# One residual subtraction of the last query head is moved ahead of the projection's evictions on VectorE

## The reference, cut to what matters

```python
def _L0_xattn_ref(query, key, value, mask, wq, wk, wv, wo):
    q = (query @ wq).reshape(bs, s, N_Q_HEADS, D_K).transpose(0, 2, 1, 3)
    k = (key @ wk).reshape(bs, s, N_KV_HEADS, D_K).transpose(0, 2, 1, 3)
    v = (value @ wv).reshape(bs, s, N_KV_HEADS, D_V).transpose(0, 2, 1, 3)
    q = _rope(q)
    k = _rope(k)
    ...
    scores = jnp.einsum('bhgqd,bhkd->bhgqk', qg, k) / scale
    masked = jnp.where(mask[:, None, None].astype(bool), scores, -1000000000.0)
    w = jax.nn.softmax(masked, axis=-1)
    out = jnp.einsum('bhgqk,bhkd->bhgqd', w, v)
    ...
    return out @ wo
```

## Time and profile before

| | |
|---|---|
| runs | 2452.93, 2455.95, 2454.99 us; median 2454.99 us |
| profiled execution | 2452.93 us, its span 2451.1 us |
| PE busy | 2382.1 us (97%) |
| PE weight load | 1309.2 us (53%) |
| DVE busy | 1636.0 us (67%) |
| ACT busy | 1254.0 us (51%) |
| POOL busy | 1221.6 us (50%) |

### The profile page before, as it was taken

The page is one execution under the profiler, slowest core; times in us unless marked ns, Lnnn a source line. Parts: engine busy times, 40 slices in busy tenths (PEclk is TensorE's granted clock), DMA queues, the critical chain, the costliest instruction groups (busy, mean ns, idle before and its releaser), DMA issues.

```text
span 2451.1 us, 45213 instructions
## 1 busy us (share of the span) xinstructions
PE 2382.1 (97%) x17719; PEld 1309.2 (53%) x17719; DVE 1636.0 (67%) x3133; ACT 1254.0 (51%) x2425; POOL 1221.6 (50%) x981
## 2 busy tenths in 40 slices
PE   7799999999999999999999999999999999999998
PEld 4455555555555555444444555555555555555554
DVE  6877777777777788754443556667666666755666
ACT  6665555555565554423232554555454555544453
POOL 3566666666666666423222355544444445445541
PEclk9899999999999999999999999999999999999999
DMA  6011211112121111101000111122221212221101
GB/s 208 27 44 35 53 44 44 39 40 53 27 53 27 42 28 41 33 20 58 28 28 12 44 31 27 27 61 55 51 61 36 61 36 61 52 42 27 27 14 69
DMA packets 221554, 108.16 MB, mean 44 GB/s; under 512 B 174080, under 2 KB 197280, under 8 KB 221344
## 3 DMA queue, kind: packets, MB, share of 16 engines
q1 hardware_dynamic: 221344, 105.27, 17.0%
HBM read 61.62 MB, written 4.19 MB: 27 GB/s over the span
## 4 chain that ended last, share of the span: by engine, by line
PE 54%; DVE 4%; POOL 3%; ACT 1%; issue 1%; DVEq 0%; ACTq 0%; POOLq 0%
PE PB L854 14%; PE PB L806 12%; PE PB L966 9%; PE PB L790 6%; PE PB L983 5%; PE PB L831 2%; PE PB L896 2%; PE PB L875 1%; DVE AR L2108 1%; DVE SML L1919 1%; PE PB L1080 1%; PE PB L925 1%; POOL AR L2720 1%; POOL PSP L2699 0%; POOL AR L2681 0%
## 5 line engine op out<-in xcount | busy, mean ns | idle before, releaser
L854 PE MATMUL PB<-WB,AR 128*128 128x512 f16 x3072 | 690.8, 381 | 16.9 <-DVE X L2123 11.2
L806 PE MATMUL PB<-XTB,WB 128*128 128x512 f16 x3072 | 682.0, 379 | 3.4 <-ACT WB L1352 1.9
L854 PEld LDWEIGHTS PB<-WB,AR 128*128 128x128 f16 x3072 | 296.7, 98 | 379.6 <-DVE X L2123 21.8
L806 PEld LDWEIGHTS PB<-XTB,WB 128*128 128x128 f16 x3072 | 299.1, 98 | 342.0 <-issue 3.1
L2692 POOL TENSOR_TENSOR AR<-AR,SML 128x512 f32<-128x512 f32 x128 | 144.6, 1151 | 316.9 <-DVE SML L2093 316.9
L2123 DVE SCALAR_TENSOR_TENSOR X<-PB,SML,X 128x512 f32<-128x512 f32 x256 | 187.3, 748 | 163.9 <-PE PB L854 157.3
L1476 ACT ACTIVATE AR<-PB 128x512 f16<-128x512 f32 x256 | 131.6, 598 | 237.9 <-PE PB L896 237.8
L2681 POOL TENSOR_TENSOR AR<-AR,CST 128x512 f32<-128x512 f32 x128 | 181.6, 1418 | 44.1 <-ACT AR L1386 44.1
L2003 DVE TENSOR_TENSOR AR<-PB,AR 128x512 f16<-128x512 f32 x128 | 88.2, 690 | 170.3 <-ACT AR L1439 170.3
L966 PE MATMUL PB<-XTB,AR 128*128 128x512 f16 (+1 forms) x864 | 192.5, 379 | 0.0
L1974 DVE TENSOR_TENSOR AR<-AR 128x512 f16<-128x512 f32 x128 | 138.7, 1083 | 69.8 <-ACT AR L1392 69.4
(11 more groups left out here) (272 smaller groups left out, 3806.4 us busy)
## 6 DMA issues: line engine op xcount, KB each, us to landing
STG<-in_wo SPq DMA_DIRECT2D x14, 1024.0 KB
STG<-in_wq SPq DMA_DIRECT2D x13, 1024.0 KB
STG<-in_qw_gu SPq DMA_DIRECT2D x40, 128.0 KB
STG<-in_ctxT SPq DMA_DIRECT2D x4, 1024.0 KB
X<-in_x SPq DMA_DIRECT2D x4, 1024.0 KB, 10.8
out_x<-X SPq DMA_DIRECT2D x16, 256.0 KB, 2.5
AR<-PSP SPq DMA_TRANSPOSE x240, 2.4
STG<-in_wk SPq DMA_DIRECT2D x14, 256.0 KB
```

The lines of the kernel that those rows point to most:

```text
L806: m = pe.do.matmul(b[:, :], wq[x][:, k, h * 128:(h + 1) * 128], XT[y][c][:, k, :], start=n == 0, stop=n == 11)
L854: m = pe.do.matmul(b[:, :], AT[x][:, h, t * 128:(t + 1) * 128], wo[y][:, h, :], start=n == 0, stop=n == 11)
```

## The change

In the program of VectorE alone, in layer 0 alone, the low part of the last query head (h = 3) of the next unit is written after the first of the four evictions instead of after the third. The side stage of that slot, which stood behind it, now stands ahead of it. Nothing is added or taken away, and no other engine's program is touched.

```diff
                         if L and t == 2:
                             norm_q(u + 1)
-                        if L == 0 and t == 2:
+                        side(L, u, 5 + t)
+                        if L == 0 and t == 0:
                             queries_0(u + 1, 3)
-                        side(L, u, 5 + t)
                     side(L, u, 9)
```

## The result

The changed kernel takes 2485.62 us (2485.04 to 2486.96, 4 runs) against 2453.96 us before (2451.37 to 2455.95): 1.0133 of the time before, 95% interval 1.012 to 1.0145, or 31.7 us more. The forecast was 2490, in the range 2478 to 2502.

The account below looks back on a forecast made before the run. TensorE was taken to bound the kernel, so only its late starts cost time. Gain 0, cost 31.2 + 4.5 = 35.7 us on the profiled 2452.9, plus 2.1 for the median, gave 2490.7; forecast 2490, range 2478 to 2502.

Parts of the forecast that it names:

- The gain, nothing: Scores of layer 0: the low part was never late for them, so gain 0, bounded by 7.6 us.
- The cost of an ordinary unit, 1.46 us: Weigh in unit 13 starts 1.46 us later, waiting for bank 0 behind the delayed evictions of tiles 1 and 2.
- The sum: Layer 0: 31.2 us from units 6 to 27 plus 4.5 us from eight other units, +35.7 us.
- Does a late weigh get hidden later? No.: TensorE after weigh: scores and keys follow back to back, so the delay is not recovered.
- What comes back to TensorE starts from TensorE's own results: Turned heads, softmax and evictions start from TensorE's results, so they slip along with a late weigh.
- rival 1: Waits at tile 3 and in unit 2 shrink to nothing, giving back 11.2 us: +24.5, 2479 us; chance 0.07.
- No second wait: Keys on bank 2: tile 3's eviction frees it with 1.4 us margin, about 1 in units with wide residuals.
- The clock: TensorE's granted clock stays 1.00 despite the new waits at weigh.
- rival 3: TensorE's clock falls at each new wait, slowing weigh and scores: 2552 us, or 2518 with weigh alone; chance 0.02.
- rival 2: Delay at weigh is hidden because its bank is free 1.46 us earlier: no change, 2455 us; chance 0.03.
- rival 4: A second wait, for bank 2, in each ordinary unit: 2502 us; chance 0.05.
- rival 5: Scores wait unseen for head 3's low part; 7.6 us gained, no cost at weigh: 2447 us; chance 0.03.

Follow-up runs that it names:

- E4: Kernel before with head 3's low part after tile 3's eviction instead of after tile 2's: 2464.24 us, 1.0041 of before.
- E2: Changed kernel with the moved instruction after tile 1's eviction instead of after tile 0's: 2468.34 us, 1.006 of before.
- E7: Kernel before with GpSimd's first sine product of the keys waiting for VectorE's softmax subtractions in rounds 10, 14, 18, 22, 26: 2452.60 us, 0.9998.
- E1: Changed kernel with tile 2 of the layer 0 projection in PSUM bank 5 instead of bank 0, output units 0 to 29: 2481.69 us, 1.0114 of before.
- E5: Changed kernel with tile 2 of the layer 0 projection in PSUM bank 5 for output units 0 to 26 only: 2475.99 us, 1.0094 of before.
- E8: Kernel before with head 2's low part put behind tile 0's eviction instead of ahead of it, rounds 1 to 30: 2443.61 us, 0.9962 of before.
- E9: Changed kernel with head 2's low part put behind tile 0's eviction as well: 2487.40 us, 1.0141 of before.

## Why the prediction was right

**What bounds the kernel.** Right for the kernel before, by TensorE's busy 743.7 of 760 us and its few waits; the chain there does not reach back into these rounds. In the changed kernel's layer 0 the chain is a loop through four engines that closes at weigh.

**The gain, nothing.** Right. The scores of layer 0 still have no wait on line 1974 in the changed kernel's rounds 6 to 27. E4 shows that they do once it is late.

**The cost of an ordinary unit, 1.46 us.** Right at its place: weigh 2.07 us after the moved instruction's start, and 22 waits of 1.35 in the mean. Over all of layer 0 weigh waits 40.6 us for evictions where it waited 3.7, so 36.9 more for the 33 to 36 foreseen. E2 takes one eviction out of the sum and the waits fall by 14.2 us, 0.65 in each of 22 rounds; the row gave 0.66.

**The sum.** Rounds 6 to 27 came to 27.4 us (681.9 - 654.6), not 31.2, and that is the term that was mis-sized: 4.2 of it in rounds 8, 10, 14, 18 and 26, which grew by 0.5 to 0.7 us in place of 1.45; rounds 6 and 22 grew by 0.7 us more than reckoned together, and round 27 by 0.2 less. In rounds 10, 14, 18 and 26 the cause is the turned order of E7, for about half of it shown and the rest argued; round 8 shows no turned order, but TensorE's wait for a small VectorE reduction (line 1869) shrinks there from 0.91 to 0.17 us. Rounds 1 to 5 came to 4.4 for 3.9. Rounds 28 to 30 came to 2.2 for 0.6: round 30 was not hidden by the unpacking as reckoned, its weigh is 1.6 us later and its scores 1.3 us. Weigh's wait grew by the 0.78 reckoned (2.00 to 2.77); beside it stands a wait that the prediction left out, of TensorE's layer norm step (line 925) for ScalarE (1485), 0.80 us that were not there before. In round 4 the same wait grew from 0.57 to 1.07, which is the excess of rounds 1 to 5. Unit 0, taken as nothing, cost 0.5. The whole came out at 34.5 us between the profiled executions, for 35.7 forecast, partly because these errors have opposite signs; that part is luck. By the medians the change is 31.7.

**"Does a late weigh get hidden later? No."** Right. "What comes back to TensorE starts from TensorE's own results": only half right, and E1 shows what it missed. Tile 0's eviction hangs on VectorE's and ScalarE's own order. In the kernel before, the heads ahead of unit 13's weigh start on ScalarE at 468.99 and those behind it at 499.41, each time at once behind another piece of its queue (one that ends at 468.96 and one at 499.38), not behind TensorE's queries. So the argument against rival 1, a chain unbroken from the queries on, was wrong, and a small part of rival 1 came true: tile 3's waits fell from 9.2 to 6.5 us, by 3.0 in rounds 10, 14, 18 and 26 alone. The prediction had them stay near 9.

**"No second wait."** Right for this kernel, and for a reason that the prediction did not give: the stall at weigh holds TensorE back so far that VectorE is in step again (2.09 us from weigh to taking up its result, 502.47 - 500.38, for 2.24 before). Take the stall away and the second way costs 19.6 us by itself (E5).

**The clock** stayed at 1.00; rival 3 did not come. Rivals 2, 4 and 5 did not either.

## What to carry to other kernels

An instruction that waits, put into an in-order queue ahead of work that is ready, costs what that work would have filled; look for the waiting instruction with ready work behind it (E8 found one in the kernel before, worth 0.4%). When a delay reaches the bounding engine by two ways, closing one gives back only what the other does not cost anyway (7.8 of 27.4 us in E5): the waits at the place that was found vanish and in large part come back elsewhere (E1, E5, E9). So before moving a bank or a buffer, ask also what the late engine does next.

## What was not expected of the hardware

A start 0.12 us earlier or 0.03 us later decides whether VectorE's subtraction (0.68 alone, 1.70 behind GpSimd) or GpSimd's product (1.27 alone, 2.39 behind VectorE) is held up, and a shift of 0.14 us against TensorE turned it in rounds 10, 14, 18 and 26. Those rounds grew by 0.8 us less than the others, of which E7 shows 0.39 to be the order; so a change of order can cost or save time at a place that it does not touch.
